# Square roots and upper parts of the weights on GpSimd, a sixth tile weighed by ScalarE and GpSimd, all calls in a new order

## The reference, cut to what matters

```python
def _layernorm(x, axis=-1, eps=1e-05):
    m = jnp.mean(x, axis=axis, keepdims=True)
    v = jnp.var(x, axis=axis, keepdims=True)
    return (x - m) / jnp.sqrt(v + eps)

# A: softmax attention over ctx_1024 (energies 256 x 256 per batch)
# B: two linear layers (256 -> 1024 -> 256, relu squared between them) whose weights are
#    quantised per block of 64: 16 scales tried, the one of least squared error kept
scale = base * s;  deq = clip(round(wb / scale), -15, 15) * scale
err = sum((deq - wb) ** 2)
# C: smooth-quantised int8 linear layers, silu between them
s = jnp.sqrt(jnp.maximum(amax_x, EPS) / jnp.maximum(amax_w, EPS))
xs = x / s;  ws = w * s            # then both rounded to +-127 with a scale per row
# D: per token and head the 8 best of 128 x 128 product keys; experts gated by silu
sim1, sim2 = q1 @ keys1, q2 @ keys2;  top_k, pair sums, top_k
out = sum_k silu(x . e_down[i_k]) * relu(score_k) * e_up[i_k]
x = x + A(ln(x));  x = x + B(ln(x));  x = x + C(ln(x));  x = x + D(ln(x))
```

## Time and profile before

| what | value |
|---|---|
| median of 3 runs | 386.91 us (386.64 to 387.16) |
| profiled execution, its own time | 388.38 us |
| its span, first to last instruction | 386.5 us |
| mean granted TensorE clock | 0.991 |
| busy share: TensorE, VectorE, ScalarE, GpSimd | 88%, 86%, 64%, 36% |
| DMA, share of 16 engines | 8.7% |

### The profile page before, as it was taken

The page is one execution under the profiler, slowest core; times in us unless marked ns, Lnnn a source line. Parts: engine busy times, 40 slices in busy tenths (PEclk is TensorE's granted clock), DMA queues, the critical chain, the costliest instruction groups (busy, mean ns, idle before and its releaser), DMA issues.

```text
span 386.5 us, 8279 instructions
## 1 busy us (share of the span) xinstructions
PE 340.7 (88%) x3222; PEld 249.5 (65%) x3222; DVE 333.8 (86%) x838; ACT 246.8 (64%) x371; POOL 140.2 (36%) x194
## 2 busy tenths in 40 slices
PE   2898796688889889999969889998999999989997
PEld 2455453243334337688948767887888887778886
DVE  3989999999989997368877999999999999999940
ACT  3899999999998992237456687755766654011000
POOL 8737524612665644211001104255424148601000
PEclk9999999999989999999998999999999999999999
DMA  8940000000000008000000000000000000000000
GB/s 252 358 137 3 1 0 0 2 0 2 2 0 0 2 1 270 2 0 3 0 2 0 3 0 3 0 3 2 2 17 16 2 15 4 2 15 2 17 15 27
DMA packets 11142, 11.40 MB, mean 29 GB/s; under 512 B 608, under 2 KB 10592, under 8 KB 11104
## 3 DMA queue, kind: packets, MB, share of 16 engines
q1 hardware_dynamic: 11104, 10.88, 8.7%
HBM read 9.83 MB, written 1.05 MB: 28 GB/s over the span
## 4 chain that ended last, share of the span: by engine, by line
DVE 46%; PE 31%; ACT 11%; issue 7%; DMA 2%; POOL 1%; SPq 1%; DVEq 0%; ACTq 0%; POOLq 0%
PE pair L934 7%; DVE arena L1663 6%; PE pair L772 5%; DVE arena L1653 4%; PE pair L626 3%; DVE i L1982 3%; DVE arena L2042 3%; PE pair L898 3%; DVE s L1976 3%; ACT arena L1200 2%; ACT arena L1203 2%; DVE arena L2038 2%; DVE XN L1588 2%; DMA arena<-in_L_ffn_keys_dram 2%; PE pair L920 2%
## 5 line engine op out<-in xcount | busy, mean ns | idle before, releaser
L1663 DVE TENSOR_REDUCE arena<-arena 128x16 f32<-128x1024 f32 x64 | 66.5, 1075 | 2.5 <-POOL arena L365 1.7
L898 PE MATMUL pair<-arena,EDT 128*128 128x256 f32 x256 | 60.2, 383 | 0.0
L934 PE MATMUL pair<-EU,arena 128*128 128x256 f32 x256 | 58.4, 382 | 0.6 <-DVE arena L2066 0.6
L934 PEld LDWEIGHTS pair<-EU,arena 128*128 128x128 f32 x256 | 47.9, 190 | 7.4 <-issue 1.0
L898 PEld LDWEIGHTS pair<-arena,EDT 128*128 128x128 f32 x256 | 47.1, 190 | 6.5 <-ACT arena L1454 0.2
L644 PE MATMUL pair<-arena,WQ 128*128 128x512 fp8e4 x112 | 33.8, 383 | 15.8 <-ACT arena L1203 7.8
L488 POOL TENSOR_TENSOR arena<-arena 128x512 f32<-128x512 f32 x20 | 27.6, 1394 | 45.1 <-ACT arena L1446 45.1
L1200 ACT ACTIVATE arena<-pair,sq_bias 128x1024 f32<-128x1024 f32 x32 | 38.4, 1199 | 2.0 <-issue 1.5
L1186 ACT ACTIVATE arena<-arena,clip_bias 128x1024 fp8e4<-128x1024 f32 x32 | 39.5, 1235 | 0.0
L656 PE MATMUL pair<-arena 128*128 128x512 fp8e4 x128 | 38.6, 384 | 1.0 <-ACT arena L1186 1.0
L1454 ACT ACTIVATE arena<-pair 128x512 f32<-128x512 f32 x32 | 19.0, 598 | 27.2 <-PE pair L898 27.1
(11 more groups left out here) (201 smaller groups left out, 666.1 us busy)
## 6 DMA issues: line engine op xcount, KB each, us to landing
arena<-in_L_ffn_e_down_dram SPq DMA_DIRECT2D x1, 2048.0 KB, 12.5
EU<-in_L_ffn_e_up_dram SPq DMA_DIRECT2D x1, 2048.0 KB, 9.2
arena<-in_L_ffn_w_fc_dram SPq DMA_DIRECT2D x2, 512.0 KB, 5.4
X<-in_x_dram SPq DMA_DIRECT2D x1, 1024.0 KB, 6.2
arena<-in_L_ffn_w_proj_dram SPq DMA_DIRECT2D x1, 1024.0 KB, 13.7
GUW<-in_fside_BxS2xS_dram SPq DMA_DIRECT2D x1, 1024.0 KB, 11.4
out_dram<-arena SPq DMA_DIRECT2D x8, 128.0 KB, 1.7
CTX<-in_ctx_dram SPq DMA_DIRECT2D x1, 512.0 KB, 4.9
```

Of the source, the lines that this page charges most:

```text
L898: last = pe.matmul(bk2(4 + i % 2)[:, r, :], EDT[:, k, at:at + P], xT4[:, b % 2, k, :], start=(k == 0), stop=(k == 1))
L934: last = pe.matmul(bk2(7)[:, n, :], PR[:, n, e, :], EU[:, e, :], start=(e == 0), stop=(e == EROWS - 1))
L1663: dve.tensor_reduce(err[:, g // NS % 2, :, g % NS], squares, AX.X, ALU.add).then_inc(s["reduced"], 1)
```

## The change

`DVE_WEIGHS` goes from 5 to 6, so tile 5 is copied out by ScalarE and weighed by GpSimd. All 13 `std` calls (one for the first norm, four each for the others), `c_root` and `c_root2` leave ScalarE, and VectorE's reciprocal of the standard deviation is gone: GpSimd adds epsilon and raises to the power -0.5, or raises the ratio to the power 0.5, with exponents from a small constant tile. `upper` of chunks 1 to 3 moves from ScalarE to GpSimd. ScalarE's opening call now uses Exp, not Identity. The lists of all four compute engines are in a new order.

```diff
+        exponents = sb("exponents", [P, 2, NT])
...
-        DVE_WEIGHS = NT - 3
+        DVE_WEIGHS = NT - 2
...
+            for i, power in enumerate((-0.5, 0.5)):
+                pool.memset(exponents[:, i, :], power)
...
+            def deviation(b, n, name):
+
+                pool.wait_ge(s[name + "_var"], b + 1)
+                r = rstd[:, n * b:n * b + n]
+                link(pool.tensor_scalar(r, mv[:, n * b:n * b + n, 1], LN_EPS, None, ALU.add))
+                pool.tensor_tensor(r, r, exponents[:, 0, 0:n], ALU.pow).then_inc(s[name + "_inv"], 1)
+
+            def c_root(b):
+
+                pool.wait_ge(s["c_ratio"], b + 1)
+                pool.tensor_tensor(sm[:, b, 1, :], tmpa[:, b, :], exponents[:, 1, 0:2], ALU.pow).then_inc(s["c_root"], 1)
+
+            def c_root2(b):
+
+                pool.wait_ge(s["c_ratio2"], b + 1)
+                pool.tensor_tensor(sm2[:, b, 1:2], t2a[:, b:b + 1], exponents[:, 1, 0:1], ALU.pow).then_inc(s["c_root2"], 1)
...
+            def upper(c):
+
+                pool.wait_ge(s["absolute"], c + 1)
+                if c >= 2:
+                    pool.wait_ge(s["diff"], NS * (c - 2) + 2)
+                pool.tensor_copy(QP[:, c % 2, 0, :], qu[:, c % 2, :]).then_inc(s["part1"], 1)
...
-            act.activation(rstd[:, 0:1], lneps[:, 0:1], ACT.Identity)
+            act.activation(esum[:, 0:1], lneps[:, 0:1], ACT.Exp)
...
-            def std(b, n, name):
-
-                act.wait_ge(s[name + "_var"], b + 1)
-                act.activation(rstd[:, n * b:n * b + n], mv[:, n * b:n * b + n, 1], ACT.Sqrt,
-                               bias=lneps[:, 0:1]).then_inc(s[name + "_std"], 1)
...
             def ln_apply(b, nt, name):
-                if nt == NT:
-                    dve.wait_ge(s[name + "_std"], 1)
-                else:
-                    dve.wait_ge(s[name + "_std"], b + 1)
-                link(dve.reciprocal(rstd[:, nt * b:nt * b + nt], rstd[:, nt * b:nt * b + nt]))
+                dve.wait_ge(s[name + "_inv"], b + 1)
...
             prepare(0)
             scale_weights(0)
-            first_stats()
             clip_round(0)
             split(0)
             clip_round(2)
             prepare(1)
-            first_inverse()
+            first_stats()
             clip_round(4)
...
-            weigh(5, (0, 1))
             top8(7)
-            weigh(5, (2,))
             pair_top8(7)
-            weigh(5, (3,))
```

More of the change, by code:

```diff
@@ L489, in weigh @@
                                        ).then_inc(s["d_weighed"], 1)
+            pool.wait_ge(s["wquant"], NCH)
+            square_hidden(8)
+            square_hidden(9)
+            deviation(0, 2, "ln3")
+            square_hidden(10)
+            c_root(0)
+            square_hidden(11)
+            square_hidden(12)
+            square_hidden(13)
+            deviation(1, 2, "ln3")
+            square_hidden(14)
+            c_root(1)
+            square_hidden(15)
+            c_root2(0)
+            deviation(2, 2, "ln3")
+            deviation(0, 2, "ln4")
+            deviation(3, 2, "ln3")
+            c_root2(1)
+            iotas()
+            c_root(2)
             ranks(0)
             coefficient_parts(0)
-            weigh(0, (0, 1, 2))
+            deviation(1, 2, "ln4")
+            weigh(0, (0,))
             ranks(1)
-            weigh(0, (3,))
+            weigh(0, (1,))
+            c_root2(2)
             coefficient_parts(1)
+            weigh(0, (2, 3))
+            deviation(2, 2, "ln4")
+            weigh(1, (0, 1))
             ranks(2)
-            weigh(1, (0, 1))
+            c_root(3)
+            weigh(1, (2, 3))
             coefficient_parts(2)
-            weigh(1, (2, 3))
             ranks(3)
+            weigh(2, (0, 1))
+            c_root2(3)
             coefficient_parts(3)
-            weigh(2, (0, 1))
+            weigh(2, (2,))
             ranks(4)
-            weigh(2, (2, 3))
+            weigh(2, (3,))
             coefficient_parts(4)
-            weigh(3, (0,))
+            deviation(3, 2, "ln4")
+            weigh(3, (0, 1, 2))
             ranks(5)
-            weigh(3, (1, 2))
+            weigh(3, (3,))
             coefficient_parts(5)
-            weigh(3, (3,))
             weigh(4, (0, 1, 2))
             ranks(6)
+            weigh(4, (3,))
             coefficient_parts(6)
-            weigh(4, (3,))
+            weigh(5, (0, 1, 2, 3))
             ranks(7)
@@ L740, in _ @@
             unit(45)
-            ffn1(3)
             unit(46)
@@ L940, in _ @@
             ffn1(8)
-            ffn1(9)
-            ffn1(10)
             pe.wait_ge(s["squared"], NU)
@@ L979, in _ @@
             c_second(0)
+            ffn2(3, 1, (0,))
             c_first(1)
@@ L1216, in _ @@
             square(1)
+            attention_inputs_out(1)
+            square(2)
             clip_round(7)
-            square(2)
+            square(3)
             exponentials(0)
-            square(3)
+            square(4)
             exponentials(1)
-            square(4)
+            square(5)
+            clip_round(9)
+            square(6)
             x_out(0)
-            square(5)
+            square(7)
             x_out(1)
-            square(6)
+            square(8)
+            clip_round(11)
@@ L1227, in _ @@
+            probs_out(0)
+            clip_round(13)
             exponentials(2)
-            probs_out(0)
-            square(7)
+            square(9)
+            x_out(2)
+            square(10)
+            absolute(1)
             probs_out(1)
-            x_out(2)
-            clip_round(9)
-            square(8)
-            absolute(1)
-            square(9)
-            clip_round(11)
-            e_down_out(0)
-            square(10)
-            exponentials(3)
-            clip_round(13)
@@ L1241, in _ @@
-            square(11)
-            upper(1)
-            square(12)
-            probs_out(2)
-            square(13)
-            clip_round(15)
-            square(14)
+            square(11)
+            square(12)
+            clip_round(15)
+            exponentials(3)
+            square(13)
+            square(14)
+            clip_round(17)
+            e_down_out(0)
+            square(15)
             x_out(3)
-            clip_round(17)
-            square(15)
-            e_down_out(1)
@@ L1263, in _ @@
+            square(22)
+            clip_round(29)
             absolute(2)
-            e_down_out(2)
-            upper(2)
-            square(21)
             e_down_out(3)
-            clip_round(25)
-            square(22)
-            std(2, 2, "ln2")
+            e_down_out(4)
             square(23)
-            clip_round(27)
+            e_down_out(5)
+            e_down_out(6)
             square(24)
-            clip_round(29)
+            clip_round(31)
             square(25)
-            e_down_out(4)
+            e_down_out(7)
@@ L1306, in _ @@
             square(39)
-            clip_round(43)
             square(40)
@@ L1754, in _ @@
             sum_error(13)
+            normalise_probabilities(3)
+            sum_error(14)
             clip_round(20)
-            sum_error(14)
             sum_error(15)
@@ L1825, in _ @@
             sum_error(51)
-            round_quantised(2)
-            clip_round(60)
+            choose(2)
             sum_error(52)
```

627 lines of the change are left out of this document (301 added, 326 removed).

## The result

The changed kernel takes 395.14 us (median of 4 runs, 394.74 to 399.45) against 386.82 us (386.64 to 387.16) for the kernel before on the same chip: ratio 1.0237, 95% interval 1.0186 to 1.0288. It is slower, clear of the noise; by the medians the ratio is 1.0215. The ratios in this document are formed from all fast runs and not from the two medians, so the two differ a little. The prediction said 381.5 us, with a range up to 391. The profiled execution took 395.05 us, its span is 393.2.

A forecast was written before the change was run, and what follows sets the result against it. VectorE and ScalarE bound it to 148 us, TensorE to 200, VectorE and TensorE to 343, then TensorE. Stages 3.4 + 0 + 2 = 5.4 us earlier, from 386.91 to 381.5 us; range 375 to 391.

The forecast's parts named there:

- Five of the nine: Nine places where VectorE idles for GpSimd's whole round trip; five (two norms, three roots) before 200 us, four behind.
- That stage: Second stage, 148 to 200 us: new waits hidden by slack, net 0, ends 2 us earlier and 3 later.
- The third stage: From 200 us: 4.3 + 1.0 saved, 2.7 + 1 lost; 2 us earlier, ends 8 earlier and 3 later.
- my 2.7: VectorE's added waiting behind 200 us: one norm at 0.9 and three roots at 0.6 us each.
- The power: A small power on GpSimd takes 0.5 us; a deviation's round trip about 0.9, a root's 0.6 us.
- The rival of the slow power: Nine pairs where nothing stands between: gain used up at 1.3 us per power, 393.5 us at 2.36; chance 0.12.
- The rival of the queue behind a wait: Roots in GpSimd's list held up behind `weigh` and `ranks`, holding VectorE: three times 2.5 us, 389 us; chance 0.06.
- The first stage: 0 to 148 us: 1.0 + 1 + 2 - 0.6 = 3.4 us earlier, ends 0 and 7.
- the 1 us named as a sign of being wrong: First stage: the units ending within 1 us of where they did would show the prediction wrong.
- the 0.6 us set for contention: First stage: a tenth more GpSimd work stretches VectorE's `clip_round` by 0.6 us more.
- the 1 + 2 us of waits: First stage, VectorE's waits removed: 1 of 2.5 us for x, 2 of 3.4 us for the units.
- The last sign of being wrong: End of the kernel: TensorE starting its last `up` less than 3 us earlier than 376.7.

The follow-up runs named there:

- number 8: Changed kernel with one move on TensorE alone: the first half of the second layer's third unit put ahead of the second unit's factors; 395.55 us, ratio 1.0227.
- experiment 4: Changed kernel with the sixth tile (tile 5) weighed by VectorE again, without GpSimd's four operations and ScalarE's four copies for it; 399.86 us, ratio 1.0328.
- number 5: Kernel before, in its old order, with only the sixth tile copied out by ScalarE and weighed by GpSimd; 388.45 us, ratio 1.0051.
- The doubling: Changed kernel with each GpSimd power of one or two columns done twice, the eight-column power once; 409.71 us, ratio 1.0574.
- experiment 1: Changed kernel with all 21 GpSimd powers made cheap, each replaced by a multiplication of two constants, order and waits kept; 388.70 us, ratio 1.0026.
- number 7: Changed kernel with VectorE's list altered at seven places after 148 us, so that other operations run beside the powers; 405.53 us, ratio 1.0492.
- experiment 10: Changed kernel in its new order on the other engines, with the 16 roots behind 148 us as square roots on ScalarE again; 405.78 us, ratio 1.0482.
- 14: All three parts of the change, with the changed kernel's order in the first stage and the kernel before's order behind it; 390.03 us, ratio 1.0067.
- 15: All three parts of the change, with the kernel before's order in the first stage and the changed kernel's order behind it; 399.10 us, ratio 1.0290.

## Why the prediction was wrong

The sum had 5.4 us earlier in the span and the span grew by 6.7, so 12.1 us are to be accounted for. They lie in all three stages: 3.0 in the first, 5.1 from `x2(0)` to `x3(0)`, 4.0 behind it. By the medians the miss is 13.6 us; the 1.5 more is what the profiled execution of the kernel before lay above its median, probably in the first stage.

**What bounds the kernel.** Right for each stage by its shares (but VectorE's third slice is an 8, not a 9), wrong in how they were used. "Five of the nine (two norms, three roots) lie before 200 us, where VectorE has 17 us of slack and TensorE has `ffn1` and `ffn2` to fill with. That stage also loses two table loads; I put it at **0**". **This is the step that failed.** From `x2(0)` to `x3(0)` the changed kernel takes 42.7 us where the kernel before took 37.6, so `x3(0)` came 4.7 us late against the 0 of the sum, and against its bad end of 3. With cheap powers the stretch takes 40.1 us: about half of the 5.1 us is the time of the powers, and the other half comes with the new order whatever a power takes.

Slack was read as VectorE's idle time. The chain of waits shows that this time was idle because small steps go back and forth between the engines beside TensorE's work, and a wait put into that chain lengthens it once the chain is the path. In the kernel before TensorE was the path there up to about 186 us; in the changed one the chain is. That this is for want of filler is argued, not shown: `ffn2(2, 0)` stood behind `c_x_transposed(1)`, and now behind `c_a_transposed(0)`, but putting it forward again in number 8 won 1.5 us in this stretch and nothing at the end.

**The third stage, "2 us earlier".** Wrong by 4: from `x3(0)` to the end it is 191.1 us against 189.1, 2 us later and not 2 earlier. The places were counted on VectorE's list alone, nine; the trace has 13 waits, as VectorE also waited at places where something stands in between. Behind 200 us VectorE waits 3.3 + 1.4 + 1.1 = 5.8 us for powers instead of my 2.7. The saving of tile 5 was right for this order: 4.3 us in the sum, 4.7 in experiment 4, and L2070 stands eight times at 1092 ns. In the old order it was no saving (number 5).

**The power.** Sized nearly right, 0.5 against 0.56 to 0.72 us; a deviation's wait is 1.14 us, not 0.9, and a root's 0.66 to 0.81, not 0.6. The rival of the slow power had the right place and sign but the wrong threshold: it reckoned with 6.5 powers in the open and a price from 1.3 us on. The doubling cost more than 16 of them, as if all of the third stage stood in the open, and even at 0.195 us a piece (experiment 1, 1.0026) the change would not have paid. The rival of the queue behind a wait came true only in number 7, which put it there.

**The first stage, "3.4 us earlier".** Wrong. The last sum of errors starts 0.9 us earlier (141.7 against 142.6) where 3 was said, within the 1 us named as a sign of being wrong. `dequantise(3)` ends 1.9 us earlier, at 148.9, but `x2(0)` starts 0.4 earlier, since TensorE now has `ffn2(1, 0)` ahead of it and VectorE waits 8.7 us there in place of 7.1. VectorE's busy time before 148 us did not fall by the reciprocals' 1.0 but rose by 2.5. `clip_round` is no worse, 841 ns against 893, its mean being worth 1.6 us. Other instructions met GpSimd instead: the application of the second normalisation takes 735 ns in place of 409, eight times, 2.6 us.

```profile
L1603 DVE TENSOR_SCALAR XN<-X,mv,rstd 128x256 f32<-128x256 f32 x8 | 5.6, 735 | 0.0
L1708 DVE TENSOR_SCALAR arena<-arena,rsum 128x256 f32<-128x256 f32 x8 | 4.6, 622 | 0.1
```

The second row is the normalisation of the probabilities, 350 ns before. That GpSimd is what stretches both is inferred from the added work, not isolated. If it is GpSimd, the 0.6 us set for contention was too small, and took up part of the 1 + 2 us of waits. The upper parts were right, 1.06 us each against 1.03.

**What held.** Two table loads; the copies and multiplications; ScalarE's busy time, 222.6 us, 24 less than the 246.8 that the stages of the earlier trace rows add up to, where 26 was said. The last sign of being wrong showed as well: the last `up` starts at 383.46, 6.8 us later than 376.70. That ScalarE could be emptied was right, but it bought little: TensorE's waits for its squares in the units fell from 15.3 to 9.2 us (L1200 and L1203 before, L1247 and L1250 after), and the units ended 0.9 us earlier.

**The load's price.** The 1.4 us per load taken from the earlier trace rows is borne out by the rows of experiment 10, where the operation behind a load starts 1.29 us after it. The Trainium skill, "ScalarE: Activation LUTs", What ACT_TABLE_LOAD costs, gives 2.66 us with the drain; no row here shows that much. What the loads cost depends more on where they stand: 2 of the 19 lie on the path in the kernel before (at 23.84 and 200.42 us), 9 of 19 in number 10.

**Still open.** Which single move of the third stage's order costs how much: it was only swapped whole (14 and 15), and the two repairs by hand failed. What the lower clock alone costs was not isolated. Why first stages differ by 1 to 2 us between executions of one kernel was not followed up.

## What to carry to other kernels

An operation moved to an idle engine is paid in latency, not in busy time: before it is moved, follow the chain of waits through the stretch and ask how much longer it may become before it is the path. An engine's idle time in a stage with a chain between engines is not slack. And a new order that is laid out for other costs has to be priced as a change of its own: swap it in alone, by stage, since here it turned one part (the tile) from +1.5 into -4.7 us and another (the powers) from nothing into most of the loss.

## What the runs showed of the hardware

**TensorE's clock falls with its gaps.** In the changed kernel TensorE stood for 2.61 us up to 184.25 and for 1.03 up to 186.44. Then (stretch, TensorE's busy time, granted clock):

```profile
185.00:186.00 1.00, 0.41 (x4) 1.00 0.09 16
186.00:187.00 1.00, 0.56 (x3) 0.67 0.00 0
187.00:188.00 1.00, 1.00 (x7) 0.50 0.02 8
...
190.00:191.00 1.00, 1.00 (x12) 1.00 0.00 0
```

That is the lower level, 1.2 of 2.4 GHz, just when the put-off `ffn2` runs: its 48 matmuls from 187.12 take 6.67 us in the chain above, those from 194.24 only 5.36. With doubled powers, after gaps of 2.65 us (up to 181.70), 2.29 and 0.85 us (up to 190.24), the same 48 take 7.91 us:

```profile
190.72 7.91 PE L832 MATMUL pair<-arena 128*128 128x128 f32 x48
```

In the version with cheap powers, after gaps of 1.27 and 1.03 us, they take 7.08 us. The next 48 take 5.52 in both versions, so the lower level is there in the new order with short powers too:

```profile
184.23 7.08 PE L827 MATMUL pair<-arena 128*128 128x128 f32 x48
```

In these traces an idle gap on the path is thus charged more than its length, and this is a part of why some 12 us of added powers cost 15.9. With the doubled powers the mean clock of the whole span fell from 0.987 to 0.962. The kernel before isn't free of it: TensorE stands for 1.31 and 1.44 us around 200 us, and from 204 to 206 us its clock is 0.50, where the changed kernel has 1.00.

**A power on GpSimd** costs by its columns: 0.56 us for 128x1, 0.71 for 128x2, 1.68 for 128x8, which makes an estimate of 0.16 us per column above a base of 0.4. A multiplication of 128x8 takes 0.20.

**A table load can run ahead of the wait.** ScalarE's load of 1.28 us runs while the operation that needs it still waits for its input. In experiment 10 a load ends at 186.82 and the root behind it starts at 187.86, having waited 1.04 us for VectorE's ratio:

```profile
185.54 1.28 ACT L1423 ACT_TABLE_LOAD   x1
187.86 0.20 ACT L1423 ACTIVATE sm<-t2a 128x1 f32<-128x1 f32 x1 [1.04 <-DVE t2a L1950]
```
